# An fp8-rounded cross-attention on one core: two float16 weight parts for three bf16 ones, and the rounding as two bf16 passes on VectorE

## The chip, the cores and the metric

The kernel runs on one core of one Trainium2 chip. The metric is the device time of one execution in microseconds (us), lower is better. A core has five engines that run their own instruction streams and meet only at semaphores: TensorE (PE in the rows; its weight loads are listed as PEld), VectorE (DVE), ScalarE (ACT), GpSimd (POOL) and SyncE (SP), which here only issues transfers.

## The reference

The program is a chain of seven blocks on 2048 tokens of width 256. The change touches one of them, a grouped-query attention whose linear layers see inputs rounded to the float8 e4m3 grid (16 query heads, 8 key groups, head width 128), once over the tokens themselves and once over a conditioning input:

```
def _div_clamp_fp8(x, scale):
    y = jnp.clip(x / scale, -FP8_MAX, FP8_MAX)
    y = y.astype(jnp.bfloat16).astype(jnp.float32)
    return _fp8_roundtrip(y)
def _fp8_linear_pertensor(x, wq, w_scale, in_scale):
    xq = _div_clamp_fp8(x, in_scale)
    return jnp.einsum('bsi,oi->bso', xq * in_scale, wq) * w_scale
...
q  = _ln(_fp8_linear_pertensor(ln_out, wq, wq_scale, q_in_scale) per head, qln_w, qln_b)
k, v, qx likewise (v without _ln);  kx, vx = split(cond @ w_kv_x.T) (kx with _ln)
cat  = concatenate([_gqa(q, k, v), _gqa(qx, kx, vx)])
catq = _div_clamp_fp8(cat, proj_smooth)
return einsum(catq, wproj) * (proj_in_scale * proj_w_scale)
```

The weights `wq`, `wqx`, `wk`, `wv` are float32. Inputs on the fp8 grid are exact in bf16, so a projection keeps float32 accuracy if the weight is split into several 16-bit parts and the products are added.

## The kernel before

The program is a list of stages, each a class with one method for each engine (`sp`, `pe`, `dve`, `act`, `pool`); a barrier of all engines stands between stages. Two stages matter here.

**The mixture-of-experts stage** (`MoeTop6`, about 392 to 582 us for its 32 experts) prepares the attention's weights beside the experts. `Fp8Weights.cuts` are 12 pieces of 128x1024. For each, SP loads the piece into `f_stage`, ScalarE scales it by input scale times weight scale (`scaled`), VectorE takes each head's mean out (`centred`; for `v` only a copy), and the piece is split into three bf16 parts: ScalarE rounds it to part 0 (`first`), VectorE subtracts (`left`), ScalarE rounds to part 1 (`second`), VectorE subtracts to part 2 (`third`). The parts lie in `w3`, which the rows print as `f_w` (numbers in names are left out). `parameters` runs on VectorE ahead of the first expert's product and makes the small vectors (scales, reciprocals).

**The attention stage** (`Fp8Attention`, about 582 to 1432 us) walks through steps `w`. In each step every engine does one unit `u` of four heads (8 units in each of 16 batches of 128 tokens, 128 units in all), each engine a different phase of it: scores of unit u on TensorE, maxima (`f_nmax`) of u-1 on VectorE, exponentials of u-1 on ScalarE, reciprocal of the sums (`sums`) of u-2 on VectorE and the division by them (`divide`, POOL line 3584) of u-2 on GpSimd, transposes of u-3, values and scaling to bf16 (`smooth`, tile `f_cb`) of u-4, rounding to the fp8 grid of u-5. Between these lie the projections of the batches to come, from the table `MADE`: in each step one "early" item (four heads of q or qx), and one "late" item, in even steps of a batch a v or vx with an output product (`o`), in odd ones a k or kx. A projected head item (kind N) goes PE product, ACT squares (`f_sq`), DVE sum of squares (`head_squares`, L3387), POOL power -1/2 (`head_factors`, L3590), DVE scaling out of PSUM (`scale_heads`, L3397), PE transposes. I number the steps of a batch 0 to 7; VectorE handles a late k or kx item of an odd step in the even step behind it. All orders are written out by hand, and each engine follows its own strictly.

The rounding adds and takes away a number 1.5 * 2^20 times the power of two of the value: the sum of a bf16 value and that number is rounded in float32 at the place where e4m3 ends. Before, `round_c` on VectorE clips (`f_cbr`), masks out the exponent (`f_cm`) and multiplies it (`f_cmr`); GpSimd adds in float32 (`round_c_pool`, L3579, tile `f_cf`); VectorE subtracts one step later (`end_c`, L3427). The tiles are laid as three rows of 172 with a gap (516 elements with padding). The same is done for each batch's 128x1024 input in `clip_z`, `round_z` on GpSimd (L3572, 2.1 us) and `end_z` (L3378). A fp8 projection (`project`) is six matmuls of 512 columns: three weight parts by two halves of the 256 inputs.

## Time and profile before

| | us |
|---|---|
| median of 3 runs | 2301.07 (2299.93 to 2303.12) |
| the profiled execution, its own time | 2299.93 |
| its span in the profile | 2298.1 |
| TensorE busy | 1964.0 (85%) |
| VectorE busy | 1788.6 (78%) |
| ScalarE busy | 1382.0 (60%) |
| GpSimd busy | 1170.5 (51%) |
| mean granted TensorE clock | 0.914 of full |

The shares are means over stages of different kinds. To see what bounds the attention stage, read busy times by stretch, then the waits, then the timeline of one batch of it. In the timeline a row is start, duration, engine, line, operation, and in brackets the idle time ahead of it with what ended it. VectorE rows overlap: an instruction that waits for nothing starts some 0.08 us ahead of the recorded end of the one before, so the time that an instruction takes of the engine is the distance of starts.

### The profile page before, as it was taken

How to read it: one execution, taken by the hardware profiler on the slowest of the kernel's cores; microseconds unless marked ns; L12 is line 12 of the kernel's file. 1: busy time of each engine (PE TensorE's matmuls, PEld its weight loads, DVE VectorE, ACT ScalarE, POOL GpSimd, SP SyncE). 2: the span in 40 equal slices, each digit the busy share in tenths (PEclk: the TensorE clock that was granted, in tenths of full speed). 3: DMA queues.
4: the chain of work that ended last, by engine and by line, in shares of the span. 5: the costliest groups of instructions: out<-in, count | busy, mean ns of one | idle time of the engine just before them, and what ended most of it. 6: DMA issues, size and time to landing. Idle time of an engine off the chain costs nothing. (4 is left out here: it accounts for less than half of the span.)

```text
span 2298.1 us, 42233 instructions
## 1 busy us (share of the span) xinstructions
PE 1964.0 (85%) x13247; PEld 1209.8 (53%) x13333; DVE 1788.6 (78%) x4005; ACT 1382.0 (60%) x3523; POOL 1170.5 (51%) x1397
## 2 busy tenths in 40 slices
PE   5999888999589999999999997499478566888878
PEld 3444455666256777676777775366244233333335
DVE  4899767575579999998999886766587698788855
ACT  0777721454278888888888887133166655477753
POOL 3444201442588888888888775132774112333310
PEclk7899979999799999999999999599599876799989
DMA  5576420776220000000000000542698301477610
GB/s 146 146 179 177 124 81 18 245 246 213 63 46 18 21 20 20 19 22 18 20 20 20 11 3 1 198 147 74 192 251 224 107 21 33 113 190 186 169 49 37
DMA packets 258180, 223.18 MB, mean 97 GB/s; under 512 B 36585, under 2 KB 237900, under 8 KB 257708
## 3 DMA queue, kind: packets, MB, share of 16 engines
q1 hardware_dynamic: 234668, 178.72, 28.0%
q0 software_dynamic: 12240, 32.39, 5.5%
q10 hardware_dynamic: 11056, 9.38, 1.3%
q8 instruction: 113, 1.85, 0.3%
q14 instruction: 103, 0.84, 0.1%
HBM read 141.98 MB, written 79.32 MB: 96 GB/s over the span
## 5 line engine op out<-in xcount | busy, mean ns | idle before, releaser
L3270 PE MATMUL bank<-f_w,f_zc 128*128 128x512 bf16 x1074 | 266.8, 383 | 26.3 <-DVE f_zc L3378 18.4
L3590 POOL TENSOR_TENSOR f_hr<-f_hr,half_pow 128x4 f32<-128x4 f32 x192 | 246.1, 1282 | 84.9 <-DVE f_hr L3387 84.8
L965 ACT ACTIVATE a_PT<-bank 128x512 f32<-128x512 f32 x384 | 214.2, 604 | 82.2 <-PE bank L719 77.7
L851 DVE TENSOR_REDUCE a_nm<-bank 128x2 f32<-128x512 f32 x384 | 242.8, 683 | 24.4 <-PE bank L712 18.2
L712 PE MATMUL bank<-a_stack_k,a_stack_q 57*128 57x256 bf16 (+1 forms) x768 | 164.3, 298 | 83.8 <-DVE a_nm L851 46.7
L3482 ACT ACTIVATE f_Pm<-bank,f_nmax 128x128 f32<-128x128 f32 x512 | 182.5, 383 | 73.7 <-DVE f_nmax L3402 73.6
L3270 PEld LDWEIGHTS bank<-f_w,f_zc 128*128 128x128 bf16 x1152 | 112.4, 99 | 121.8 <-issue 25.6
L965 ACT ACTIVATE f_w<-bank 128x512 f32<-128x512 f32 x256 | 141.4, 600 | 46.9 <-PE bank L719 36.3
L851 DVE TENSOR_REDUCE f_w<-bank 128x2 f32<-128x512 f32 x256 | 162.5, 682 | 8.6 <-PE bank L712 7.1
L3397 DVE TENSOR_TENSOR f_raw<-bank,f_hr 128x512 f32<-128x512 f32 x192 | 131.5, 685 | 42.8 <-POOL f_hr L3590 42.8
L3579 POOL TENSOR_TENSOR f_cf<-f_cbr,f_cmr 128x516 f32<-128x516 bf16 x128 | 156.9, 1226 | 12.6 <-DVE f_cb L3427 11.0
L3387 DVE TENSOR_REDUCE f_hr<-f_sq 128x4 f32<-128x516 f32 x192 | 131.3, 684 | 38.7 <-ACT f_sq L3517 36.8
L3494 ACT ACTIVATE f_cb<-bank,f_rsmooth 128x128 bf16<-128x128 f32 x512 | 147.2, 378 | 23.8 <-PE bank L3230 23.8
L719 PE MATMUL bank<-a_stack_q,a_stack_k 60*128 60x256 bf16 (+1 forms) x768 | 154.9, 282 | 6.1 <-ACT a_PT L965 5.6
L1915 POOL DMA_INDIRECT m_xe<-moe_in,m_token x64 | 75.6, 1181 | 164.8 <-DVE m_token L1794 80.9
L3517 ACT ACTIVATE f_sq<-bank 128x512 f32<-128x512 f32 x192 | 116.5, 607 | 62.4 <-PE bank L3270 38.7
L712 PEld LDWEIGHTS bank<-a_stack_k,a_stack_q 57*128 57x128 bf16 (+1 forms) x768 | 59.0, 100 | 178.9 <-DVE a_nm L851 115.0
L3584 POOL TENSOR_TENSOR f_Pm<-f_Pm,f_rs 128x512 f32<-128x512 f32 x128 | 132.6, 1036 | 23.3 <-DVE f_rs L3407 23.3
L3219 PEld LDWEIGHTS bank<-f_KT,f_QT 128*128 128x128 f32 x1024 | 129.3, 192 | 19.9 <-issue 10.5
L3219 PE MATMUL bank<-f_KT,f_QT 128*128 128x128 f32 x1024 | 135.2, 275 | 0.0
L3230 PE MATMUL bank<-f_PT,f_Vv 128*128 128x256 f32 x512 | 132.1, 381 | 2.3 <-ACT f_cb L3494 2.3
L1133 POOL DMA_INDIRECT f_rows<-moe_out,slot x96 | 107.5, 1119 | 45.8 <-ACTq L137 29.8
(410 smaller groups left out, 5108.4 us busy)
## 6 DMA issues: line engine op xcount, KB each, us to landing
o<-a_sums SPq DMA_DIRECT2D x32, 512.0 KB
cut<-a_parts SPq DMA_DIRECT2D x64, 192.0 KB
cut<-a_parts SPq DMA_DIRECT2D x96, 128.0 KB
m_w<-in_w SPq DMA_DIRECT2D x32, 368.0 KB
moe_out<-m_oe ACTq DMA_DIRECT2D x32, 256.0 KB
cut<-f_w SPq DMA_DIRECT2D x32, 192.0 KB, 3.5
cut<-f_w SPq DMA_DIRECT2D x48, 128.0 KB, 2.7
f_w<-cut SPq DMA_DIRECT2D x32, 192.0 KB, 3.6
```

The lines of the kernel that those rows point to most:

```text
L712: x = t.matmul(ps[:, n * D:(n + 1) * D], self.stack_q[rows, i, slot, n * P:(n + 1) * P], self.stack_k[rows, i, slot, :], start=True, stop= ...
L719: x = t.matmul(ps[:, n * D:(n + 1) * D], self.stack_k[rows, i, slot, n * P:(n + 1) * P], self.stack_q[rows, i, slot, :], start=True, stop= ...
L851: v.tensor_reduce(self.nm[:, g % 2, :, at % self.J, at // self.J], self.k.bank[h % 3][:, :].rearrange("p (n m) -> p n m", n=2), AX.X, ALU. ...
L965: a.activation(self.PT[:, h % 8, :, :].rearrange("p m n -> p (m n)"), self.k.bank[3 + h % 3][:, :], ACT.Exp).then_inc(self.a_exp.sem, 1)
L3219: x = t.matmul(ps[:, j * P:(j + 1) * P], self.QT[:, cross, h, :], self.KT[:, cross, h // 2, :], start=True, stop=True)
L3230: x = t.matmul(self.k.bank[7][:, j * 2 * P:(j + 1) * 2 * P], self.Vv[:, cross, n * 2 + j, :], self.PT[:, u % 2, j * 2 * P:(j + 1) * 2 * P] ...
L3270: x = t.matmul(ps[:, :], self.zc[:, b % 2, j, c_, :], self.fp8.w3[:, m, c_, at:at + BANK], start=(m == 0 and c_ == 0), stop=(m == 2 and c_ ...
L3482: x = a.activation(self.Pm[:, i, j * P:(j + 1) * P], ps[:, j * P:(j + 1) * P], ACT.Exp, bias=self.nmax[:, i, j:j + 1], accum_out=self.rs[: ...
L3494: x = a.activation(self.cb[:, u % self.NCB, j * P:(j + 1) * P], ps[:, j * P:(j + 1) * P], ACT.Copy, scale=self.fp8.rsmooth[:, h:h + 1])
L3579: g.tensor_tensor(self.cf[:, :].rearrange("p (r n) -> p r n", r=3), clipped, steps, ALU.add).then_inc(self.g_c.sem, 1)
L3584: g.tensor_tensor(pm, pm, self.rs[:, u % 3, :].unsqueeze(2).to_broadcast([P, self.HPB, P]), ALU.mult).then_inc(self.g_P.sem, 1)
L3590: g.tensor_tensor(f, f, self.k.half_pow[:, 0:self.HPB], ALU.pow).then_inc(self.g_hr.sem, 1)
```

## The change

1. **Weights as two float16 parts.** `w3` (three bf16 parts) becomes `cut_w` (two float16 parts, a third less memory). Each piece loses `left` on VectorE (float32 128x1024) and `second` on ScalarE; `rest` has two buffers for three. A projection is four matmuls for six.
2. **Scaling for float16's range.** `parameters` also loads the input scales as rows (`in_rows`, one more transfer, 512 KB), finds the largest factor of each projection, divides by it and multiplies by 32; the constant under the square root (`least_sq`) is scaled for each kind of head, so `sq` gets a region for each of the four kinds; the scaling of v is taken back in `rsmooth`.
3. **Rounding on VectorE alone, in bf16.** The number added is now 24 times the exponent (in bf16 the sum has 8 bits, which ends where e4m3 does), the addition and the subtraction are bf16 `tensor_tensor` instructions on VectorE, tiles `f_cs`, `f_zs`. GpSimd's additions, their waits, and `end_c` one step later are gone. The tiles are plain 128x512; the five instructions are handed out over the step by a generator (`yield`), between the other work.
4. Memory of the first attention moves (a new tile `spare`), with no instruction added or moved there.

The core of the diff:

```
-            for m in range(3):
+            for m in range(2):
                 for c_ in range(DC):
-                    x = t.matmul(ps[:, :], self.zc[:, b % 2, j, c_, :], self.fp8.w3[:, m, c_, at:at + BANK],
-                                 start=(m == 0 and c_ == 0), stop=(m == 2 and c_ == DC - 1))
+                    x = t.matmul(ps[:, :], self.zc[:, b % 2, j, c_, :], self.fp8.cut_w[:, m, c_, at:at + BANK],
+                                 start=(m == 0 and c_ == 0), stop=(m == 1 and c_ == DC - 1))
...
+    def second(self, v, n):
         v.wait_ge(self.a_w0.sem, self.a_w0.at(n + 1))
-        v.tensor_tensor(x, x, self.part(n, 0), ALU.subtract).then_inc(self.v_rest.sem, 1)
...
+        v.tensor_tensor(self.part(n, 1), self.rest[:, n % 2, :], self.part(n, 0), ALU.subtract).then_inc(self.v_w1.sem, 1)
...
+            c.mark(v.tensor_scalar(self.in_rows[:, j, :], self.in_rows[:, j, :], ws[:, j:j + 1], None, ALU.mult))
...
+        c.mark(v.tensor_reduce(most[:, :], self.in_rows[:, :, :], AX.X, ALU.max, apply_absolute_value=True))
...
+            rounding = self.round_c(v, u - 5) if self.on(u - 5) else iter(())
             if self.on(u - 1):
                 self.maxima(v, u - 1)
+            next(rounding, None)
...
     def round_c(self, v, u):
...
+        at = c.mark(v.tensor_scalar(x, x, FP8_MAX, -FP8_MAX, ALU.min, ALU.max))
+        yield
+        c.after(at)
+        at = c.mark(v.tensor_scalar(m.bitcast(U16), x.bitcast(U16), 0x7F80, None, ALU.bitwise_and))
+        yield
+        c.after(at)
+        at = c.mark(v.tensor_scalar(m, m, 2.0 ** -6, self.GRID, ALU.max, ALU.mult))
+        yield
+        c.after(at)
+        at = c.mark(v.tensor_tensor(sums, x, m, ALU.add))
+        yield
+        c.after(at)
+        v.tensor_tensor(x, sums, m, ALU.subtract).then_inc(self.v_cb.sem, 1)
+        yield
...
+        c.mark(v.tensor_tensor(zs, zb, zm, ALU.add))
+        c.after()
+        v.tensor_tensor(zb, zs, zm, ALU.subtract).then_inc(self.v_z.sem, 1)
...
-    def round_c_pool(self, g, u):
-        g.wait_ge(self.v_cm.sem, self.v_cm.at(u + 1))
-        if u:
-            g.wait_ge(self.v_cb.sem, self.v_cb.at(u))
-        clipped, steps = self.rows_of(u)
-        g.tensor_tensor(self.cf[:, :].rearrange("p (r n) -> p r n", r=3), clipped, steps, ALU.add).then_inc(self.g_c.sem, 1)
```

**VectorE, one even step of a batch in the middle of the attention stage, before.** It has a late k or kx item; `f_nmax` opens the step.

```order
L3402 TENSOR_REDUCE f_nmax<-bank 128x4
L3397 TENSOR_TENSOR f_raw<-bank,f_hr 128x512
L3387 TENSOR_REDUCE f_hr<-f_sq 128x4
L3407 RECIPROCAL f_rs<-f_rs 128x4
L3413 TENSOR_SCALAR f_cbr<-f_cb 128x3x172
L3415 TENSOR_SCALAR f_cm<-f_cbr 128x516
L3417 TENSOR_SCALAR f_cmr<-f_cm 128x3x172
L3397 TENSOR_TENSOR f_raw<-bank,f_hr 128x512
L3387 TENSOR_REDUCE f_hr<-f_sq 128x4
L3427 TENSOR_TENSOR f_cb<-f_cf,f_cmr 128x516
```

The same step after. `f_cs` holds the bf16 sums.

```order
L3414 TENSOR_REDUCE f_nmax<-bank 128x4
L3424 TENSOR_SCALAR f_cb<-f_cb 128x512
L3409 TENSOR_TENSOR f_raw<-bank,f_hr 128x512
L3427 TENSOR_SCALAR f_cm<-f_cb 128x512
L3399 TENSOR_REDUCE f_hr<-f_sq 128x4
L3430 TENSOR_SCALAR f_cm<-f_cm 128x512
L3419 RECIPROCAL f_rs<-f_rs 128x4
L3409 TENSOR_TENSOR f_raw<-bank,f_hr 128x512
L3433 TENSOR_TENSOR f_cs<-f_cb,f_cm 128x512
L3399 TENSOR_REDUCE f_hr<-f_sq 128x4
L3436 TENSOR_TENSOR f_cb<-f_cs,f_cm 128x512
```

Between the late item's `f_hr` and the `f_raw` that needs its power from GpSimd stood four instructions; two are left there (one multiplication and the reciprocal). The two passes for the sum stand around the early item's `f_hr`, behind that `f_raw`.

**GpSimd, an even step (4) and the odd one behind it, before** (`f_Pm` is the division, `f_hr` the power, `f_rows` a gather):

```order
L3579 TENSOR_TENSOR f_cf<-f_cbr,f_cmr 128x516
L3590 TENSOR_TENSOR f_hr<-f_hr,half_pow 128x4
L3584 TENSOR_TENSOR f_Pm<-f_Pm,f_rs 128x512
L3590 TENSOR_TENSOR f_hr<-f_hr,half_pow 128x4
L1133 DMA f_rows<-moe_out,slot 128x256
L3579 TENSOR_TENSOR f_cf<-f_cbr,f_cmr 128x516
L3584 TENSOR_TENSOR f_Pm<-f_Pm,f_rs 128x512
L3590 TENSOR_TENSOR f_hr<-f_hr,half_pow 128x4
```

After:

```order
L3579 TENSOR_TENSOR f_hr<-f_hr,half_pow 128x4
L3573 TENSOR_TENSOR f_Pm<-f_Pm,f_rs 128x512
L3579 TENSOR_TENSOR f_hr<-f_hr,half_pow 128x4
L1134 DMA f_rows<-moe_out,slot 128x256
L3573 TENSOR_TENSOR f_Pm<-f_Pm,f_rs 128x512
L3579 TENSOR_TENSOR f_hr<-f_hr,half_pow 128x4
```

The additions into `f_cf` are gone, and the division follows the late item's power directly.

**TensorE, an even step, before** (`f_w` is the weight tile):

```order
L3219 MATMUL bank<-f_KT,f_QT 128x128 x4
L3270 MATMUL bank<-f_w,f_zc 128x512 x6
L3198 MATMUL bank<-ident,f_Pm 128x128 x4
L3230 MATMUL bank<-f_PT,f_Vv 128x256 x2
L3206 MATMUL bank<-ident,f_raw 128x128 x4
L3263 MATMUL bank<-f_wkv,f_cT 128x512 x2
L3251 MATMUL bank<-f_wproj,f_cb 128x256 x8
```

After:

```order
L3229 MATMUL bank<-f_KT,f_QT 128x128 x4
L3280 MATMUL bank<-f_cut_w,f_zc 128x512 x4
L3208 MATMUL bank<-ident,f_Pm 128x128 x4
L3240 MATMUL bank<-f_PT,f_Vv 128x256 x2
L3216 MATMUL bank<-ident,f_raw 128x128 x4
L3273 MATMUL bank<-f_wkv,f_cT 128x512 x2
L3261 MATMUL bank<-f_wproj,f_cb 128x256 x8
```

The order is the same; the projection has four matmuls for six.

## Rows read from the trace of the kernel before

**Rows 1.** Busy us by stretch; columns: stretch, length, engines, granted clock, DMA share, GB/s
```profile
392.00:582.00 190.00, 181.75 (x792) 126.10 (x792) 111.75 (x162) 79.88 (x132) 75.56 (x64) 1.00 0.70 221
...
689.00:1289.00 600.00, 588.68 (x3512) 421.59 (x3572) 544.89 (x1237) 498.56 (x1596) 519.99 (x445) 1.00 0.08 20
...
1339.00:1387.00 48.00, 47.51 (x284) 34.06 (x288) 38.35 (x78) 40.21 (x131) 32.96 (x29) 1.00 0.00 1
1387.00:1432.00 45.00, 36.47 (x231) 28.22 (x230) 32.21 (x75) 32.98 (x126) 24.70 (x23) 0.94 0.00 1
```

**Rows 2.** Timeline: one batch input's last rounding pass, twelve batches apart
```profile
688.95 1.22 DVE L3378 TENSOR_TENSOR f_zc<-f_rows,f_zm 128x1024 bf16<-128x1024 f32 x1
...
1289.38 1.22 DVE L3378 TENSOR_TENSOR f_zc<-f_rows,f_zm 128x1024 bf16<-128x1024 f32 x1
```

**Rows 3.** Timeline: a whole projection of six matmuls, merged
```profile
940.49 1.46 PE L3270 MATMUL bank<-f_w,f_zc 128*128 128x512 bf16 x6 [0.64 <-DVE f_zc L3378]
```

**Rows 4.** Waits, 689 to 1289 us; columns: us in total, times, longest
```profile
DVE f_raw L3397 <- POOL f_hr L3590: 27.9, 36, 1.2
...
DVE f_hr L3387 <- ACT f_sq L3517: 15.5, 24, 1.0
```

**Rows 5.** Timeline of step 0, an even step, from the late item's squares on
```profile
933.70 0.68 DVE L3387 TENSOR_REDUCE f_hr<-f_sq 128x4 f32<-128x516 f32 x1
...
934.38 0.39 DVE L3413 TENSOR_SCALAR f_cbr<-f_cb 128x516 bf16<-128x516 bf16 x1
934.74 1.17 POOL L3579 TENSOR_TENSOR f_cf<-f_cbr,f_cmr 128x516 f32<-128x516 bf16 x1
...
935.87 1.01 POOL L3590 TENSOR_TENSOR f_hr<-f_hr,half_pow 128x4 f32<-128x4 f32 x1
936.87 1.03 POOL L3584 TENSOR_TENSOR f_Pm<-f_Pm,f_rs 128x512 f32<-128x512 f32 x1
936.92 0.69 DVE L3397 TENSOR_TENSOR f_raw<-bank,f_hr 128x512 f32<-128x512 f32 x1 [1.23 <-POOL f_hr L3590]
937.53 0.68 DVE L3387 TENSOR_REDUCE f_hr<-f_sq 128x4 f32<-128x516 f32 x1
938.12 0.69 DVE L3427 TENSOR_TENSOR f_cb<-f_cf,f_cmr 128x516 bf16<-128x516 f32 x1
938.29 1.39 POOL L3590 TENSOR_TENSOR f_hr<-f_hr,half_pow 128x4 f32<-128x4 f32 x1 [0.39 <-DVE f_hr L3387]
938.73 0.48 DVE L1140 SCALAR_TENSOR_TENSOR X<-f_rows,wts,X 128x256 f32<-128x256 f32 x1
```

**Rows 6.** Timeline of step 1, an odd step: its first instruction, and the one behind L3427
```profile
940.26 0.68 DVE L3402 TENSOR_REDUCE f_nmax<-bank 128x4 f32<-128x512 f32 x1
...
944.35 0.48 DVE L1140 SCALAR_TENSOR_TENSOR X<-f_rows,wts,X 128x256 f32<-128x256 f32 x1
```

**Rows 7.** Timeline of step 3: a subtraction that starts while GpSimd divides
```profile
954.56 1.04 POOL L3584 TENSOR_TENSOR f_Pm<-f_Pm,f_rs 128x512 f32<-128x512 f32 x1
955.07 1.09 DVE L3427 TENSOR_TENSOR f_cb<-f_cf,f_cmr 128x516 bf16<-128x516 f32 x1
```

**Rows 8.** Groups by shape: prices of bf16 passes; columns: busy us, mean ns, idle ahead
```profile
L1773 DVE TENSOR_SCALAR f_w<-f_w 128x384 bf16<-128x384 bf16 x4 | 0.8, 255 | 0.0
...
L3365 DVE TENSOR_SCALAR f_zc<-f_zc 128x1024 bf16<-128x1024 bf16 x1 | 0.4, 421 | 0.0
```

**Rows 9.** One line's instructions, durations ns min/median/max: the last feed-forward's matmuls
```profile
L2874 PE MATMUL bank<-t_xs,w_L_w x192: 379/379/634, 2210.1 to 2284.3; 128*128 128x512 f16 x192
```

**Rows 10.** Timeline of step 1, ScalarE: the late item's squares
```profile
945.63 0.68 ACT L3517 ACTIVATE f_sq<-bank 128x512 f32<-128x512 f32 x1
```

**Rows 11.** Timeline, expert stage: a gather on GpSimd with a copy on VectorE inside it
```profile
528.40 1.55 POOL L1915 DMA_INDIRECT m_xe<-moe_in,m_token  x1 [2.69 <-PE bank L1576]
529.14 0.69 DVE L1239 COPY f_rest<-f_stage 128x1024 f32<-128x1024 f32 x1
```

**Rows 12.** Timeline: VectorE's first product behind the parameters
```profile
405.43 0.88 DVE L1819 TENSOR_TENSOR m_he<-m_sge,bank 128x256 f32<-128x256 f32 x2 [5.70 <-PE bank L1590]
```

More of the change, by code:

```diff
@@ L1168, in allocate_staging @@
         s = lambda name, n: self.k.sb(f"f_{name}", [P, n, self.STG], F32, ctx)
-        self.stage, self.rest = s("stage", 2), s("rest", 3)
+        self.stage, self.rest = s("stage", 2), s("rest", 2)
         self.mean = self.k.sb("f_mean", [P, 2, self.STG // HD1], F32, ctx)
@@ L1211, in parameters @@
         for j in range(4):
-            c.mark(v.tensor_scalar(self.wins[:, j, :], self.ins[:, j, :], ws[:, j:j + 1], None, ALU.mult))
+            c.mark(v.tensor_scalar(self.in_rows[:, j, :], self.in_rows[:, j, :], ws[:, j:j + 1], None, ALU.mult))
+            c.mark(v.tensor_scalar(self.wins[:, j, :], self.ins[:, j, :], ws[:, j:j + 1], W_TOP, ALU.mult, ALU.mult))
+        c.after()
+        c.mark(v.tensor_reduce(most[:, :], self.in_rows[:, :, :], AX.X, ALU.max, apply_absolute_value=True))
+        c.after()
+        c.mark(v.tensor_scalar(most[:, :], most[:, :], FLT_MIN, None, ALU.max))
+        c.after()
+        c.mark(v.tensor_scalar(self.rsmooth[:, 0:HEADS1], self.rsmooth[:, 0:HEADS1], most[:, 3:4], 1.0 / W_TOP, ALU.mult, ALU.mult))
+        c.after()
+        c.mark(v.reciprocal(most[:, :], most[:, :]))
+        c.after()
+        c.mark(v.tensor_tensor(self.least_sq[:, :], most[:, :], most[:, :], ALU.mult))
+        for j in range(4):
+            c.mark(v.tensor_scalar(self.wins[:, j, :], self.wins[:, j, :], most[:, j:j + 1], None, ALU.mult))
+        c.after()
+        c.mark(v.tensor_scalar(self.least_sq[:, 0:3], self.least_sq[:, 0:3], HD1 * EPS * W_TOP * W_TOP, None, ALU.mult))
+        c.mark(v.memset(self.least_sq[:, 3:4], HD1 * EPS))
         for at in (0, 4):
@@ L1658, in dve @@
             if not odd and 0 <= n - 2 < len(self.fp8.cuts):
-                self.fp8.left(v, n - 2)
-            if odd and 0 <= n - 3 < len(self.fp8.cuts):
-                self.fp8.third(v, n - 3)
+                self.fp8.second(v, n - 2)
             if odd and 0 <= n < len(self.fp8.cuts):
@@ L1854, in act @@
             n, odd = divmod(e - 2, 2)
-            if odd and 0 <= n - 2 < len(self.fp8.cuts):
-                self.fp8.second(a, n - 2)
             if not odd and 0 <= n - 1 < len(self.fp8.cuts):
@@ L3282, in dve @@
             u = w - self.PRE
+            rounding = self.round_c(v, u - 5) if self.on(u - 5) else iter(())
             if self.on(u - 1):
                 self.maxima(v, u - 1)
+            next(rounding, None)
             for x in self.early(w - 1):
                 self.scale_heads(v, x)
+            next(rounding, None)
             for x in self.made.get(w - 1, []):
@@ L3336, in prepare @@
         if b is not None:
-            self.clip_z(v, b)
-        b = self.batch(w, self.ROUNDED)
-        if b is not None:
-            self.end_z(v, b)
+            self.round_z(v, b)
     def moments(self, v, b, src):
@@ L3386, in head_squares @@
         v.wait_ge(self.a_sq.sem, self.a_sq.at(n + 1))
-        v.tensor_reduce(self.factors(item), self.sq[:, n % self.NSQ, :, :], AX.X, ALU.add).then_inc(self.v_hv.sem, 1)
+        v.tensor_reduce(self.factors(item), self.squares(item), AX.X, ALU.add).then_inc(self.v_hv.sem, 1)
     def scale_heads(self, v, item):
@@ L3516, in square @@
             a.wait_ge(self.v_hv.sem, self.v_hv.at(n - self.NSQ + 1))
-        a.activation(self.sq[:, n % self.NSQ, :, 0:HD1], self.bank_of[item][:, :].rearrange("p (h d) -> p h d", h=self.HPB),
+        a.activation(self.squares(item)[:, :, 0:HD1], self.bank_of[item][:, :].rearrange("p (h d) -> p h d", h=self.HPB),
                      ACT.Square).then_inc(self.a_sq.sem, 1)
@@ L3557, in pool @@
                 self.power(g, b, 1)
-            b = self.batch(w, self.CLIPPED)
-            if b is not None:
-                self.round_z(g, b)
     def power(self, g, b, n):
@@ L3618, in program @@
                         first.allocate_tail(rest)
+                        spare = k.sb("spare", [P, 5120], F32, rest)
                     experts.allocate()
```

124 lines of the change are left out of this document (50 added, 74 removed).

## The prediction

> **What bounds the kernel now.** I read first the table of stretches, then the waits of the attention stage, then the timeline of one of its batches. The attention stage takes 582 to 1432 us; nearly all that the change does for time lies there. In its regular part, 689 to 1289 us, TensorE is busy 588.7 of 600 us, VectorE 544.9, GpSimd 520.0, ScalarE 498.6, at a granted clock of 1.00 [rows 1]. The same instruction comes at 688.95 and 1289.38 with eleven between: 12 batches, **50.04 us a batch** [rows 2]. TensorE looks like the bound. But VectorE's gaps are few and named: 27.9 us for GpSimd's power of a late item and 15.5 us for ScalarE's squares [rows 4], or 2.3 and 1.3 us a batch. VectorE overlaps neighbours by some 0.08 us, so its busy time (45.4 a batch) and these waits and its short waits for its own results make up the whole 50. Two engines are full, and a change that relieves one has to be counted through the other.
>
> **TensorE.** Six matmuls of 512 columns take 1.46 us of which the last one's own 0.38 is not pitch: (1.46 - 0.38) / 5 = 0.216 us each [rows 3]. The change takes 2 of 6 from 12 projections a batch: 24 x 0.216 = 5.2 us. TensorE alone would then need at most 50.0 - 5.2 = **44.8 us a batch**. float16 moving data costs the same: 379 ns a matmul of the same shape [rows 9].
>
> **VectorE, the prices.** I count from start to start. A 512-element float32 pass takes 0.68 and 0.60 of pitch (937.53 to 938.12) [rows 5]. The three bf16 passes of one input lose the odd layout: 384 elements take 0.255 and 1024 take 0.421 [rows 8], so 512 take 0.29, pitch 0.20, where 516 in three rows take 0.39 [rows 5]. The new two-input bf16 pass has no row. Bounds: 0.29 (the one-input pass) and 0.69 (L3427 in float32) [rows 5, 8]. I take 0.42, pitch 0.34, because L3413, 16 bit in a layout that can't be halved, runs 516 elements in 0.39. For the 1024 form the same way 0.69 (between 0.42 and 1.22 [rows 2, 8]).
>
> The Trainium skill (VectorE: DVE Perf Modes, § The perf-mode tier table) says that a bf16 `tensor_tensor` from SBUF does two elements a cycle; an estimate by it is 0.27 us and the fixed part of some 0.15, 0.42. No run here shows it yet.
>
> **An even step** (step 0). Before, without waits: maxima and early scaling 1.20, then from the late item's sum of squares to the end of the rounding 938.73 - 933.70 = 5.03, less the wait of 1.23, 3.80 [rows 5]; 5.00 a step, 20.0 for four, and 2.3 + 1.3 of waits [rows 4]: 23.6. After: maxima 0.60, clip 0.20, early scaling 0.60, mask 0.20; now the late sum of squares starts, call it 0. The multiplication and the reciprocal end at 0.9. But the late scaling waits for the power on GpSimd, which starts 0.76 after the sum of squares does (937.53 to 938.29) and takes 1.01 (935.87) [rows 5]: it ends at 1.77, the scaling starts at 1.81 and the next could at 2.41. Before, the 1.2 us of rounding covered this latency; **the change takes the cover away**, while it also takes GpSimd's 1.17 us addition out of its way. From 1.77 to 2.80 GpSimd divides (1.03, directly behind the power as at 936.87 [rows 5]). Here the trace has a second cost: a VectorE pass with two SBUF inputs that starts inside the division does not run: 955.07 took 1.09 instead of 0.69, and ended 0.56 after the division's end [rows 7], 0.13 less than its free duration. So the bf16 addition ends at 2.80 + 0.30 = 3.10, the next starts at 3.02; early sum of squares 0.60, bf16 subtraction 0.34: 3.96. Step: 1.60 + 3.96 = 5.56, four 22.2. The wait for ScalarE's squares stays in part: in step 1 they end at 945.63 + 0.68 = 6.05 after that step's maxima [rows 6, 10], with the shorter odd step VectorE asks at 5.9; I keep 0.8 of the 1.3. Together 23.0, a gain of **0.6**.
>
> **An odd step** (step 1). Before: 944.35 - 940.26 = 4.09 [rows 6], four and the stall of 0.4 in step 3 [rows 7]: 16.8. After: 0.60 + 0.20 + 0.60 + 0.20 + 0.40 (output added) + 0.20 = 2.20 up to the reciprocal. From its start: the bf16 addition runs 0.12 to 0.54, ahead of the division, which it holds back: behind a VectorE pass of this kind GpSimd ends 0.87 after the pass does (938.12 + 0.69 = 938.81, 938.29 + 1.39 = 939.68) [rows 5]; so about 1.44. The sum of squares (0.60) runs beside it, then the subtraction is held: it ends 1.74, the next starts 1.66. Step 3.86, four 15.4: a gain of **1.4**.
>
> **The rest of a batch.** The input's rounding: two passes of pitch 0.73 and 0.61 and one more wait for an own result (0.1) against 1.14 of L3378: **-0.3**. The tokens are ready one step earlier and GpSimd's 2.1 us are gone; nobody waits long for either. Sum: 0.6 + 1.4 - 0.3 = 1.7; the other odd and even steps carry some own-result waits that the new order spreads out, which I put at 0.15: **1.85 us a batch, 48.2**. ScalarE (41.5 a batch [rows 1]) and GpSimd (43.3 less 8 x 1.17 and 2.1, 32) stay below. TensorE, with 44.8, waits in gaps under a microsecond; I expect its clock to stay at 1.00.
>
> **Outside the regular part.** The stretch 1339 to 1387 has no input to prepare: VectorE is busy 38.4 of 48, TensorE 47.5 [rows 1], and it has the full 72 projection matmuls, so it follows TensorE's 5.2 down until ScalarE (40.2) binds: 4. The last unit run, 1387 to 1432, is a chain of rounding (1.3 us of bf16 passes, 1.17, 0.69, two waits in place of which come 1.8): 2. The fill, 582 to 643, is latency: three passes, GpSimd's 2.1 and L3378's 1.2 give way to 1.4, and the first projections have four matmuls: 3. The stretch 643 to 689: 2. In the expert stage VectorE loses 12 passes of 1.2 us and ScalarE 12 of 1.0, but TensorE is busy 181.8 of 190 us there [rows 1]: 0. `parameters` grows by four 256-element passes (0.3 each), a reduction of 1024 (1.2) and some ten small ones with waits, 4.9 us; VectorE idles 5.70 us ahead of its first product [rows 12]: covered, by less than 1 us. The row load of 512 KB is issued while no transfer is urgent: 0.
>
> **Sum** against the profiled execution: 2299.93 - 13 x 1.85 - 4 - 2 - 3 - 2 = 2299.93 - 35 = 2265. That execution stands 1.1 us under the median of 2301.07: 2266; I say **2265**.
>
> **Rivals.**
> *TensorE binds (20%).* If the new passes are not held by the division, and the power comes sooner, the VectorE batch is 48.2 less the holds, (0.27 + 0.29) x 4 = 2.3, and less the squares' wait, 45.1: TensorE's 44.8 decides. 13 x 5.2 + 5 + 5 + 2 + 6 = 86 at most: 2215. For it: TensorE's share; against: the 1.09 us row [rows 7].
> *The two-input pass runs at float32's rate (7%), slower.* At 0.69 in place of 0.42 each of 16 passes adds 0.26 to its step, and the holds don't absorb it, since they end with the division: 4.2, and the two input passes 1.1: 53.5 a batch, 13 x 3.4 = 45 longer, less 7 outside: 2338. It decides from about 0.52 us a pass (18 x 0.1 eats the 1.85).
> *Gathers hold the clip and the mask (5%), slower.* Six gathers of 1.1 us a batch lie where these two now run. If a gather held VectorE's one-input passes of the halved kind as the division holds L3427, the mask would wait some 0.5 us six times: 51.2 a batch, 2300 + 15 - 9 = 2306. Against it: the copy at 529.14, 1024 float32 elements in 0.69 where a full-rate pass needs 1.22, ran inside a gather at its usual time [rows 11].
> The Trainium skill (SBUF — State Buffer, § Who interferes with whom) states the general rule, a two-port VectorE mode and GpSimd exclude each other for the whole instruction; a page's rule that would give this rival's time. The copy's row does not show it for a gather.
> *Gain and new waits cancel (10%)*: ScalarE's squares and the power come later than I laid them by 0.25 a step: 2296 to 2304.
> Forecast case: 58%, 2245 to 2290.
>
> **How the numbers follow.** Range 2215 to 2302: it leaves out the slower cases and the edge of the TensorE one, some 20%. A difference under 0.2% is about what a measurement of this kernel can't tell from none. Faster by more: 58 + 20 = 78%; within: 10%; slower: 12%.
>
> **What would show it.** Right: 48 us between two input roundings; TensorE busy about 93% of them at clock 1.00; the bf16 addition near 0.42 free and up to 0.8 where it starts inside a division; a wait of `f_raw` for `f_hr` of some 0.8 us four times a batch; no GpSimd addition. Wrong: TensorE still 98% busy (then the division doesn't hold), two-input passes at 0.68, clips above 0.3 us beside gathers, or VectorE's first product later than 405.4 us.

## The result, and the profile after

| | before | after |
|---|---|---|
| median, us | 2302.1 (4 runs, 2299.93 to 2306.65) | **2270.83** (4 runs, 2259.74 to 2274.26) |
| ratio | | **0.984**, 95% interval 0.981 to 0.988 |
| the profiled execution, its span | 2299.93, 2298.1 | 2274.26, 2272.5 |
| mean granted clock of it | 0.914 | 0.902 |
| attention stage, from the start of its first `memset` to the start of the last addition into X | 848.3 | **816.7** |
| one regular batch | 50.04 | **48.46** |

2265 was predicted, 2215 to 2302 as the range. Busy time by stretch, columns as in [rows 1]: the regular part, and the two stretches at the stage's end.

```profile
690.00:1272.00 582.00, 536.81 (x3296) 393.26 (x3295) 531.95 (x1345) 485.01 (x1597) 360.51 (x336) 1.00 0.08 20
...
1319.00:1367.00 48.00, 47.19 (x296) 35.23 (x295) 39.05 (x95) 43.64 (x145) 23.84 (x22) 1.00 0.00 1
1367.00:1409.00 42.00, 35.93 (x232) 27.76 (x230) 36.08 (x89) 34.00 (x129) 11.85 (x10) 1.00 0.00 1
```

TensorE is busy 92% of the regular part, where it was 98% [rows 1], VectorE 91%. The end of a batch input's rounding, timeline of VectorE, eleven batches apart:

```profile
739.04 0.69 DVE L3388 TENSOR_TENSOR f_zc<-f_zs,f_zm 128x1024 bf16<-128x1024 bf16 x1
...
1272.13 0.69 DVE L3388 TENSOR_TENSOR f_zc<-f_zs,f_zm 128x1024 bf16<-128x1024 bf16 x1
```

(1272.13 - 739.04) / 11 = 48.46 us a batch, against 50.04 [rows 2]. VectorE's waits between 690 and 1272 us (us in total, times, longest), which answer to [rows 4]:

```profile
DVE f_raw L3409 <- POOL f_hr L3579: 41.3, 48, 0.9
DVE f_hr L3399 <- ACT f_sq L3527: 4.4, 12, 0.4
```

Four times in each of 12 batches VectorE waits 0.83 to 0.88 us for GpSimd's power: 3.4 us a batch, where it was 2.3. The waits for the squares fell from 1.3 to 0.4. An even step from the late item's power on, timeline of GpSimd and VectorE, as [rows 5]:

```profile
984.33 1.01 POOL L3579 TENSOR_TENSOR f_hr<-f_hr,half_pow 128x4 f32<-128x4 f32 x1 [4.48 <-DVE f_hr L3399]
...
985.31 1.03 POOL L3573 TENSOR_TENSOR f_Pm<-f_Pm,f_rs 128x512 f32<-128x512 f32 x1
985.37 0.69 DVE L3409 TENSOR_TENSOR f_raw<-bank,f_hr 128x512 f32<-128x512 f32 x1 [0.83 <-POOL f_hr L3579]
985.97 0.65 DVE L3433 TENSOR_TENSOR f_cs<-f_cb,f_cm 128x512 bf16<-128x512 bf16 x1
...
987.15 0.41 DVE L3436 TENSOR_TENSOR f_cb<-f_cs,f_cm 128x512 bf16<-128x512 bf16 x1
```

The bf16 addition starts inside the division (985.31 to 986.34) and ends 0.28 behind it, at 986.62; the subtraction, free, takes 0.41. The odd step and the start of the even one behind it:

```profile
990.18 0.43 DVE L3433 TENSOR_TENSOR f_cs<-f_cb,f_cm 128x512 bf16<-128x512 bf16 x1
990.31 1.19 POOL L3573 TENSOR_TENSOR f_Pm<-f_Pm,f_rs 128x512 f32<-128x512 f32 x1 [1.89 <-DVE f_rs L3419]
...
991.22 0.57 DVE L3436 TENSOR_TENSOR f_cb<-f_cs,f_cm 128x512 bf16<-128x512 bf16 x1
...
992.83 1.12 POOL L1134 DMA_INDIRECT f_rows<-moe_out,slot  x1 [0.18 <-issue]
...
993.50 0.54 DVE L3427 TENSOR_SCALAR f_cm<-f_cb 128x512 uint16<-128x512 uint16 x1
```

Here the addition comes first and lengthens the division (1.19 for 1.03), and the subtraction meets it. The last row was not in my main sum: a mask takes 0.54 instead of 0.28 and ends 0.09 behind a gather's end (993.95). In twelve batches 24 of 96 masks and 24 of 96 clips do so, four passes a batch. All of them start 0.43 to 0.46 us ahead of a gather's end. A clip that starts earlier in a gather, and a mask that starts still later, run free:

```profile
999.07 1.09 POOL L1134 DMA_INDIRECT f_rows<-moe_out,slot  x1 [0.18 <-issue]
999.27 0.28 DVE L3424 TENSOR_SCALAR f_cb<-f_cb 128x512 bf16<-128x512 bf16 x1
...
1000.08 0.28 DVE L3427 TENSOR_SCALAR f_cm<-f_cb 128x512 uint16<-128x512 uint16 x1
```

**Ahead of the attention stage the profiled execution of the changed kernel lost 10 us** (the stage starts at 592.2, before at 582.3). The stretch is one that the diff doesn't touch. The same kernel was profiled again (e10 below). One stretch of both profiles, first that of the table above, then e10's:

```profile
270.00:335.00 65.00, 56.18 (x290) 35.33 (x282) 30.94 (x95) 21.53 (x37) 2.80 (x3) 0.53 0.34 110
```

```profile
270.00:335.00 65.00, 55.63 (x337) 37.41 (x336) 40.92 (x124) 22.31 (x39) 2.59 (x3) 0.74 0.34 109
```

At a granted clock of 0.53 (nearly all of it at 1.2 GHz) against 0.74 the second had done more of its work by 335 us, and its attention stage started at 579.4. Over the 14 profiled executions of this case the stage started nine times at 579 to 582 us, with a granted clock of 0.71 to 0.76 between 270 and 335 us, and five times at 589 to 592, with 0.53 to 0.56; the changed kernel is in both groups. So medians of few runs carry some 10 us that no kernel made, and below I read the attention stage and the batch first: they repeat (48.46 and 48.49 us, 816.7 and 815.9).

### The profile page after: what moved, and what is told of

It is laid out like the page before. It is cut to its first block and busy times, and to the rows that moved or that the text cites. A ratio compares the mean times of both kernels' runs of the same rounds, so it can differ in the third digit from the quotient of the medians.

```text
span 2272.5 us, 41321 instructions
## 1 busy us (share of the span) xinstructions
PE 1915.8 (84%) x12949; PEld 1178.3 (52%) x12949; DVE 1763.4 (78%) x4155; ACT 1355.3 (60%) x3511; POOL 959.4 (42%) x1253
## 5 line engine op out<-in xcount | busy, mean ns | idle before, releaser
L3579 POOL TENSOR_TENSOR f_hr<-f_hr,half_pow 128x4 f32<-128x4 f32 x192 | 215.4, 1122 | 192.1 <-DVE f_hr L3399 191.6
L3280 PE MATMUL bank<-f_cut_w,f_zc 128*128 128x512 f16 x768 | 202.5, 388 | 14.0 <-DVE f_raw L3409 7.8
L3573 POOL TENSOR_TENSOR f_Pm<-f_Pm,f_rs 128x512 f32<-128x512 f32 x128 | 142.6, 1114 | 111.9 <-DVE f_rs L3419 111.9
L966 ACT ACTIVATE f_cut_w<-bank 128x512 f32<-128x512 f32 x256 | 141.7, 600 | 51.6 <-PE bank L720 41.0
L852 DVE TENSOR_REDUCE spare<-bank 128x2 f32<-128x512 f32 x256 | 162.4, 681 | 8.8 <-PE bank L713 7.4
L3504 ACT ACTIVATE f_cb<-bank,f_rsmooth 128x128 bf16<-128x128 f32 x512 | 153.7, 431 | 5.2 <-PE bank L3240 3.5
L3216 PE MATMUL bank<-ident,f_raw 128*128 128x128 f32 x768 | 114.8, 277 | 42.4 <-ACT f_PT L3484 41.3
L3527 ACT ACTIVATE f_sq<-bank 128x512 f32<-128x512 f32 x192 | 121.1, 631 | 43.8 <-PE bank L3273 22.1
L3273 PE MATMUL bank<-f_wkv,f_cT 128*128 128x512 f32 x256 | 123.2, 606 | 6.2 <-DMA f_cT<-in_ctx_T 5.9
L3216 PEld LDWEIGHTS bank<-ident,f_raw 128*128 128x128 f32 x768 | 91.3, 142 | 69.3 <-issue 55.9
```

The source lines that it names most:

```text
L852: v.tensor_reduce(self.nm[:, g % 2, :, at % self.J, at // self.J], self.k.bank[h % 3][:, :].rearrange("p (n m) -> p n m", n=2), AX.X, ALU. ...
L966: a.activation(self.PT[:, h % 8, :, :].rearrange("p m n -> p (m n)"), self.k.bank[3 + h % 3][:, :], ACT.Exp).then_inc(self.a_exp.sem, 1)
L3216: x = t.transpose(ps[:, h * P:(h + 1) * P], self.raw[:, n % self.NRAW, h * HD1:(h + 1) * HD1], self.k.ident[:, :])
L3280: x = t.matmul(ps[:, :], self.zc[:, b % 2, j, c_, :], self.fp8.cut_w[:, m, c_, at:at + BANK], start=(m == 0 and c_ == 0), stop=(m == 1 and ...
L3504: x = a.activation(self.cb[:, u % self.NCB, j * P:(j + 1) * P], ps[:, j * P:(j + 1) * P], ACT.Copy, scale=self.fp8.rsmooth[:, h:h + 1])
L3573: g.tensor_tensor(pm, pm, self.rs[:, u % 3, :].unsqueeze(2).to_broadcast([P, self.HPB, P]), ALU.mult).then_inc(self.g_P.sem, 1)
```

## Experiments

Batch, stage and median of all (batch: between two input roundings in the regular part; ratio to the kernel before on the same chip):

| kernel | batch | stage | median | ratio, 95% |
|---|---|---|---|---|
| before | 50.04 | 848.3 | 2302.1 | |
| changed | 48.46 | 816.7 | 2270.8 | 0.984 (0.981 to 0.988) |
| e1 weight parts, GpSimd rounds the output | 49.73 | 832.7 | 2287.1 | 0.995 (0.992 to 0.998) |
| e2 six matmuls | 49.29 | 836.5 | 2291.0 | 0.994 (0.990 to 0.997) |
| e3 two matmuls | 48.5 / 50.1 | 819.2 | 2270.7 | 0.989 (0.982 to 0.995) |
| e4 short division (part of the work left out) | 47.20 | 799.4 | 2246.3 | 0.977 (0.971 to 0.982) |
| e5 passes in the power's shadow | 46.68 | 792.7 | 2242.7 | 0.974 (0.970 to 0.977) |
| **e6 passes ahead of the reciprocal** | **45.97** | **783.1** | **2232.7** | **0.969** (0.965 to 0.972) |
| e7 = e6, six matmuls | 48.92 | 831.7 | 2279.5 | 0.991 (0.986 to 0.996) |
| e8 = e6, two matmuls | 45.9 / 46.9 | 785.4 | 2234.5 | 0.973 (0.967 to 0.980) |
| e9 early reciprocal | 47.00 | 795.5 | 2239.3 | 0.972 (0.969 to 0.975) |
| e10 changed, again | 48.49 | 815.9 | 2269.6 | 0.987 (0.983 to 0.990) |
| e11 plain rows for gathers (other rows) | 48.23 | 809.9 | 2252.4 | 0.978 (0.975 to 0.982) |
| e12 = e6, plain rows (other rows) | 45.74 | 776.9 | 2222.4 | 0.966 (0.961 to 0.970) |

My theory, theory A in the expectations: VectorE's chain, with its waits for GpSimd, sets the batch on both sides of the change. The first rival, theory B: TensorE set it, and the weight parts carry the gain.

### e1, e2, e3: each part alone, and TensorE's load

e1 is the changed kernel with `round_c`, `end_c` and `round_c_pool` of before:

```diff
-            rounding = self.round_c(v, u - 5) if self.on(u - 5) else iter(())
+            if self.on(u - 5):
+                self.round_c(v, u - 5)
...
+            if self.on(u - 6):
+                self.end_c(v, u - 6)
```

> The change with the rounding of the attention's output as before the change (three one-input passes in three rows, addition on GpSimd, L3427-type subtraction in float32); the two float16 weight parts and the rounding of the inputs on VectorE stay. Theory A (VectorE's chain sets the batch, TensorE only waits for it): a batch of 49.3 to 49.8 us, since VectorE gets back its passes and keeps only the 0.3 us of the inputs' rounding and a part of the 1.3 us of waiting for ScalarE's squares; 2283 us (2278 to 2292). Theory B (the weight parts carry the gain, TensorE was the bound): 44.8 to 46.5 us a batch, 2225 to 2247 us.

49.73 us a batch: theory A. With 24 matmuls fewer in each batch TensorE was busy 91% and the batch hardly moved.

e2 and e3 change only the parts' loop in `project`, and the `stop` flag of its last matmul with it (the comments are mine):

```diff
-            for m in range(2):
+            for m, last in ((0, False), (1, False), (1, True)):   # e2
+            for m in range(1):                                    # e3
```

> The changed kernel with six matmuls a projection instead of four: the second weight part is multiplied twice, so TensorE has its load of before the change and VectorE the new rounding (the projections come out a rounding error of the weights off). TensorE is now busy 461.2 of 500 us, 44.7 us a batch of 48.46; 24 more matmuls of 0.216 us are 5.2: 49.9. If both engines stand at the edge as I hold, the batch becomes 50 us and the kernel about 2297 us (2292 to 2303): the new rounding alone would be worth nearly nothing. If TensorE were far from binding even then: 48.5 us and 2271 us.

49.29, 0.6 to 0.7 less than expected, with TensorE full; the median of 2291 stands just under the expected range. The regular part (700 to 1200 us) of e2, and of e7, which has the same matmuls in the better order:

```profile
700.00:1200.00 500.00, 498.86 (x3026) 356.76 (x3024) 447.20 (x1134) 422.59 (x1352) 305.26 (x285) 1.00 0.07 20
```

```profile
700.00:1200.00 500.00, 500.00 (x3047) 360.27 (x3046) 450.12 (x1148) 425.49 (x1362) 302.39 (x287) 1.00 0.08 20
```

TensorE is shown busy all the time in both, at 49.29 and at 48.92 us a batch, so busy time alone doesn't give its need. With six matmuls that need is at most e7's **48.92 us**, 1.1 under the 50.04 of before: VectorE's chain was the longer of two nearly equal ones. The rounding alone can give no more than the distance between them (e2: 0.75), the weight parts alone only what VectorE lets through (e1: 0.31, and that came with the inputs' rounding on VectorE), together 1.58. That is 0.5 more than the two gains added. Some 0.3 of it is the longer rounding of the inputs, which e1 and e2 both carry and the whole carries once; only about 0.2 is left for each part uncovering the other engine. e6 and e7 below show that effect at its full size.

> The changed kernel with two matmuls a projection: the second weight part is left out of the product. TensorE would need 39.5 us a batch. Theory A (VectorE's chain with its waits for GpSimd sets 48.46): 48.2 to 48.5 us a batch, and only the stretch without inputs to prepare and the fill get shorter, 2260 to 2271 us. Theory B (TensorE still sets the pace by when it delivers): 43 to 46 us a batch, 2200 to 2240 us.

Seven of the twelve batches took 48.47, five 50.1. VectorE's chain stands, theory A; but the emptier TensorE cost time. Stretches of one of the long batches, and VectorE's wait behind them:

```profile
902.00:904.50 2.50, 0.39 (x5) 0.40 (x5) 2.50 (x8) 2.50 (x11) 1.00 (x1) 1.00 0.19 56
904.50:907.00 2.50, 2.50 (x10) 1.41 (x9) 2.50 (x6) 2.14 (x6) 2.31 (x3) 0.63 0.00 0
907.00:909.50 2.50, 2.50 (x11) 1.45 (x10) 0.53 (x2) 0.94 (x4) 0.13 (x1) 0.68 0.18 52
```

```profile
909.19 0.69 DVE L3399 TENSOR_REDUCE f_hr<-f_sq 128x4 f32<-128x516 f32 x1 [1.97 <-ACT f_sq L3527]
```

TensorE was busy 0.39 of 2.5 us, its granted clock then averaged 0.63 and 0.68 (in part at 1.2 GHz, in part at 2.4), the projection came late, and VectorE waited 1.97 us for its squares. Each of the five long batches has one such drop, 3.4 us at 1.2 GHz, and none of the seven short ones has. The stage took 819.2 us, longer than with twice the matmuls, and the median is the changed kernel's.

### e4: what the division holds

```diff
-        g.tensor_tensor(pm, pm, self.rs[:, u % 3, :].unsqueeze(2).to_broadcast([P, self.HPB, P]), ALU.mult).then_inc(self.g_P.sem, 1)
+        g.tensor_tensor(pm[:, :, 0:1], pm[:, :, 0:1], self.rs[:, u % 3, :].unsqueeze(2), ALU.mult).then_inc(self.g_P.sem, 1)
```

> The changed kernel with GpSimd's division of the probabilities cut to one element of 128 in each head (the other probabilities stay undivided; that part of the computation is left out), all waits kept. Theory A (a two-input bf16 pass that meets the division waits for its end, and GpSimd's power of an early item queues behind it): the additions of the even steps and the subtractions of the odd steps fall from about 0.65 to 0.42, and their queues with them, 8 times 0.24 to 0.29, or 1.9 to 2.3 us a batch: 46.2 to 46.6 us a batch, 2240 to 2248 us. Rival (these passes are long for another reason, such as ScalarE's traffic): their durations stay at 0.65 and the batch at 48.0 to 48.5, 2265 to 2271 us.

Durations (ns, min/median/max) of the bf16 addition and subtraction, one line's view each, were 424/537/665 and 407/562/664; now:

```profile
L3433 DVE TENSOR_TENSOR f_cs<-f_cb,f_cm x84: 412/421/427, 704.4 to 1193.8; 128x512 bf16<-128x512 bf16 x84
```

```profile
L3436 DVE TENSOR_TENSOR f_cb<-f_cs,f_cm x84: 411/416/419, 705.3 to 1194.8; 128x512 bf16<-128x512 bf16 x84
```

The division took 0.19 to 0.36 us instead of 1.03 to 1.19, and the passes are free: the hold is the division's. The batch fell by 1.26, not 1.9 to 2.3: the surplus durations were 4 x 0.23 and 4 x 0.15 to 0.25, 1.6 in all, and waiting for the squares grew from 3.6 to 8.0 us in 500, 0.4 a batch.

### e5, e6: the cover given back

In e6 the addition and the subtraction stand behind the multiplication and ahead of the reciprocal. e5 has them behind the reciprocal.

```diff
             for x in late:
                 self.head_squares(v, x)
             next(rounding, None)
+            next(rounding, None)
+            next(rounding, None)
             if self.on(u - 2):
                 self.sums(v, u - 2)
             for x in late:
                 self.scale_heads(v, x)
-            next(rounding, None)
             for x in self.early(w):
                 self.head_squares(v, x)
-            next(rounding, None)
```

> The changed kernel with both two-input bf16 passes moved between the reciprocal and the scaling of the late item, same work. In the changed kernel's batch VectorE waits 0.83 to 0.88 us four times for the power of the late item, and runs the addition and the subtraction (0.34 each) behind that wait. Theory A (the wait is what the lost cover costs): the two passes fill it, and the held additions (0.22 us more each, even steps) go too, since they now start ahead of the division: 4 x (0.8 + 0.2), 4 us less a batch, but not under TensorE's 44.7: 44.7 to 46 us a batch instead of 48.46, 2220 to 2237 us on this chip. Rival (GpSimd's power is itself held by the VectorE passes beside it and comes later by what they take): the wait comes back, 47.5 to 48.5 us a batch, 2258 to 2271 us. Second rival: the subtractions of the odd steps, now directly behind the additions, meet the division and hold everything behind them: 46.5 to 47.5.

> As the run with both two-input bf16 passes moved ahead of the late scaling, but they stand ahead of the reciprocal too, so that in no step a division can run beside them. Theory A: no pass is held (all at 0.42), the wait of 0.83 us for the power is covered; against it the division starts 0.7 us later in each step, and who waits for the divided probabilities gets them later. 44.7 to 46 us a batch if that has slack (GpSimd is busy 63%), 2218 to 2237 us; 47 to 48.5 us and 2250 to 2271 us if the late division moves the power of the early item, which queues behind it, onto VectorE's path.

An even step of e6, from the power on:

```profile
966.86 1.01 POOL L3579 TENSOR_TENSOR f_hr<-f_hr,half_pow 128x4 f32<-128x4 f32 x1 [4.09 <-DVE f_hr L3399]
967.01 0.43 DVE L3433 TENSOR_TENSOR f_cs<-f_cb,f_cm 128x512 bf16<-128x512 bf16 x1
967.48 0.43 DVE L3436 TENSOR_TENSOR f_cb<-f_cs,f_cm 128x512 bf16<-128x512 bf16 x1
...
967.91 0.69 DVE L3409 TENSOR_TENSOR f_raw<-bank,f_hr 128x512 f32<-128x512 f32 x1
968.07 1.04 POOL L3573 TENSOR_TENSOR f_Pm<-f_Pm,f_rs 128x512 f32<-128x512 f32 x1 [0.20 <-DVE f_rs L3419]
```

Both passes run while GpSimd computes the power, and the late scaling follows without a wait. The work of this even step took 4.61 us, in the changed kernel 5.52. e5 gains the same there, but its 46.68 missed the 44.7 to 46 of its theory and fell in the range of its second rival. It loses in the odd steps, where the subtraction meets the division (1.15 us for 0.43):

```profile
977.62 1.19 POOL L3573 TENSOR_TENSOR f_Pm<-f_Pm,f_rs 128x512 f32<-128x512 f32 x1 [1.69 <-DVE f_rs L3419]
977.94 1.15 DVE L3436 TENSOR_TENSOR f_cb<-f_cs,f_cm 128x512 bf16<-128x512 bf16 x1
```

In e6 the division of an odd step meets the addition of a gathered row instead (0.91 for 0.47 us, three times a batch), the smaller loss: 45.97, at the upper end of the 44.7 to 46 expected. It is the fastest kernel here that computes all of the reference: 1.6% under the changed kernel by the two ratios (1.8% by e10's), 3.2% under the kernel before.

### e7, e8: what binds e6

> The order with both two-input bf16 passes ahead of the reciprocal (45.97 us a batch), with six matmuls a projection: the second weight part is multiplied twice, so TensorE has its load of before the change. With this load the changed kernel took 49.29 us a batch with TensorE busy 498.9 of 500 us. Theory (that was TensorE's own need): again 49.2 to 49.4 us a batch, 12 x 3.3 us and some 10 us outside longer than the 2233 us of this order, 2278 to 2290 us; the weight parts are then worth 3.3 us a batch here and 0.8 in the change's order. Rival (49.29 was made of both engines' waits for each other): the better order shows here too, 47.5 to 48.7 us a batch, 2255 to 2270 us.

> The order with both two-input bf16 passes ahead of the reciprocal, with two matmuls a projection: the second weight part is left out. Theory (VectorE's own work, busy 483.8 of 500 us, now sets 45.97 us a batch, and TensorE's 96% busy is waiting with it): 45.8 to 46.0 us a batch where the granted clock stays at 1.00, up to 1.6 more in batches where it falls, as in the run with one product in the change's order; 2222 to 2240 us. Rival (TensorE has become the bound): 42 to 44.5 us a batch, under 2215 us.

e7 gave 48.92, between the theory (49.2 to 49.4) and the rival (47.5 to 48.7): most of e2's 49.29 was TensorE's need, and 0.37 of it came from the order. With the better order the weight parts are worth 2.95 us a batch, in the change's own order 0.83 (49.29 - 48.46). e8 gave 45.95 in four batches and 46.9 in eight, each with 3.4 us at 1.2 GHz. With two matmuls fewer a projection the short batches are no shorter than e6's: VectorE's own work binds e6.

### e9: an attempt that lost

In odd steps the reciprocal moves up behind the clip, and the subtraction stays behind the early sum of squares; even steps have e5's order. The cut shows the reciprocal's move.

```diff
+            if not late and self.on(u - 2):
+                self.sums(v, u - 2)
             for x in self.early(w - 1):
                 self.scale_heads(v, x)
```

> The changed kernel in the order of the first better one in the even steps (both two-input bf16 passes between the reciprocal and the late scaling), and in the odd steps the reciprocal moved up behind the clip, so that the division starts some 2 us earlier and runs beside passes that read PSUM, the subtraction behind the early sum of squares. Theory (in the order with the passes ahead of the reciprocal the division of an odd step holds the addition of a gathered row behind it, 0.91 instead of 0.47 us three times a batch, and once the 0.40 us pass of L3336, 0.77): 45.97 - 3 x 0.44 - 0.37 = 44.3 us a batch, but TensorE's own need is 44.3 to 44.7 too, so 44.5 to 45.1; 13 times 1.2 less than 2232.7, 2213 to 2222 us. Rival (ScalarE's exponentials of the row come too late for an early reciprocal, and VectorE waits there): 46 us a batch or more, 2232 us.

47.00 us a batch and 2239 us, a miss for the theory, and the rival's cause isn't it either. ScalarE wasn't waited for; the mask, a pass of one input, met GpSimd:

```profile
987.55 1.09 POOL L1134 DMA_INDIRECT f_rows<-moe_out,slot  x1 [0.18 <-issue]
...
988.46 1.96 DVE L3431 TENSOR_SCALAR f_cm<-f_cb 128x512 uint16<-128x512 uint16 x1
988.68 0.58 POOL L3572 TENSOR_TENSOR f_mv<-f_mv,half_pow 128x1 f32<-128x1 f32 x1
989.23 1.04 POOL L3577 TENSOR_TENSOR f_Pm<-f_Pm,f_rs 128x512 f32<-128x512 f32 x1
```

It waited through the gather's end, a small power and the whole division: 1.96 us instead of 0.28. With only the division beside it the mask took 0.65 to 1.09, the more the earlier in the division it started. I had counted only passes of two inputs as held.

### e10, e11, e12: the loss ahead of the stage, and the gathers

> The changed kernel once more, beside the kernel before on another chip. Its attention stage should again take 817 us (48.46 us a batch); if the 10 us that the profiled run of it lost ahead of that stage belong to the run and not to the kernel, its attention stage may start at 580 us here as well as at 592, and the median should stand some 30 us under that of before (2265 to 2275); if they belong to the kernel, it starts at 592 again.

The stage started at 579.4: the 10 us belong to the run.

In e11 and e12 plain transfers of fixed rows take the place of the gathers, so these two compute with other rows than the reference does:

```diff
-        at = bass.IndirectOffsetOnAxis(ap=self.slot[:, b, j:j + 1], axis=0)
-        g.indirect_dma_start(rows[:, j, :], None, self.k.obuf, at, bounds_check=SLOTS, oob_is_err=False).then_inc(self.d_row[j].sem, 16)
+        g.dma_start(rows[:, j, :], self.k.obuf[(j + 1) * P:(j + 2) * P, :]).then_inc(self.d_row[j].sem, 16)
```

> The changed kernel with GpSimd's indirect gathers of expert rows (1.07 to 1.12 us each, six a batch) replaced by plain transfers of 128 rows from the same queue; the rows are others, so the input of the attention is, too. Theory (of the 192 clips and masks in 12 batches 48 take 0.53 instead of 0.28, each of them started in the last 0.5 us of a gather: the gather holds them): all clips and masks take 0.28, and a batch gets up to 4 x 0.25 = 1.0 us shorter, less what comes back as waiting for ScalarE's squares (up to 0.4): 47.4 to 47.9 us a batch, 2256 to 2263 us. Rival (they are long for another reason, or lie under the waits for GpSimd's power): 48.3 to 48.5 us a batch, 2268 to 2271 us.

> The order with both two-input bf16 passes ahead of the reciprocal (45.97 us a batch), with plain transfers in place of the gathers (other rows). There the clips and masks that meet a gather lose only 0.05 to 0.08 us, some three times a batch each: 45.6 to 45.9 us a batch by the durations. If GpSimd, 6.6 us a batch emptier, also lets the division of the odd steps end earlier, the held additions of rows (0.91 instead of 0.47) may shorten: down to 45.0. Slower than 46 if the emptier GpSimd only moves its divisions under other VectorE passes.

The mask in the changed kernel, and in e11:

```profile
L3427 DVE TENSOR_SCALAR f_cm<-f_cb x83: 275/281/540, 702.7 to 1199.2; 128x512 uint16<-128x512 uint16 x83
```

```profile
L3426 DVE TENSOR_SCALAR f_cm<-f_cb x83: 274/280/288, 704.6 to 1199.5; 128x512 uint16<-128x512 uint16 x83
```

So the long masks and clips were the gathers' doing. But the batch gained only 0.23, since in the even steps, where three of the four stood, the waits for ScalarE's squares came back: 3.6 us in 500 before, 11.4 now. 48.23 lies just under the rival's 48.3 and above the theory's 47.4 to 47.9: the durations were as the theory had them, the price was not. e12 gave 45.74, the middle of what the durations said. The stages of e11 and e12 are 6.8 and 6.2 us shorter, of which 13 x 0.23 explains 3; another 1.7 and 2.3 lie between the first two input roundings, and why is open.

## Why the prediction was right, point by point

**The sum.** 35 us were predicted as 24 in the regular part and 11 outside; the stage gave 31.6, of which 13 x 1.58 = 20.5 in the regular part and 11.1 outside. That the outside comes out is in part luck, since its terms don't. Measured between the maxima that open the batches (`f_nmax`), the fill up to the first of them was 5.3 us shorter (3 predicted), the next stretch 2.4 us longer (2 shorter predicted), the last stretch with an input 2.9 shorter (1.85), the one without an input 3.7 shorter (4), and the rest of the stage 3.2 shorter (2).

**The batch** gained 1.58 us for 1.85. One batch of each kernel, divided at the end of each step's own work (what follows is preparation of inputs and the gathered rows):

| | before | after | gain | predicted |
|---|---|---|---|---|
| four even steps | 23.7 | 23.4 | 0.3 | 0.6 |
| four odd steps | 17.1 | 15.6 | 1.5 | 1.4 |
| the rest | 9.2 | 9.5 | -0.25 | -0.3 |
| own-result waits | | | in the rows above | 0.15 |

**The prices held.** The two-input bf16 pass takes 0.41 to 0.43 free (0.42 taken between bounds of 0.29 and 0.69), the one of 1024 elements 0.69, the one-input pass 0.28 (0.29). The rival at float32's rate is dead. The estimate by the Trainium skill (VectorE: DVE Perf Modes, § The perf-mode tier table) was 0.42 too; the trace agrees.

**TensorE.** 24 matmuls were priced at 5.2 us; by busy time it was 49.1 - 44.7 = 4.4 a batch. "At most 50.0" for TensorE alone is now at most 48.92 (e7). Its clock stayed at 1.00 in the regular part, as said. That it doesn't bind the changed kernel is shown by e3: half its projection matmuls gone, and the batches without a drop of the clock still take 48.47. That six matmuls would have bound a quicker VectorE is shown by e7.

**Even steps.** Predicted 22.2 and 0.8 of waiting for squares, 23.0; the four took 5.52, 5.84, 5.76 and 6.27 up to the next work of `prepare`, 23.4. The power's wait (0.83 to 0.88), the hold by the division (end 0.28 behind it, 0.30 taken) and the clean step of 5.52 (5.56) are as worked out. Three of the four passes held by gathers lie in these steps, 0.26 us each, and the waiting for squares fell to 0.4 us a batch, not 0.8.

**Odd steps.** Predicted 15.4, measured 3.84, 3.84, 4.09 and 3.83: 15.6. The 4.09 is one clip held by a gather. The four of before took 17.1, not the 16.8 of the sum, which took step 1 four times and 0.4 for the stall in step 3: that step took 4.71, 0.6 more than step 1, and step 7 took 4.22.

**The inputs' rounding** cost 0.3 more, as said. "Nobody waits long" for GpSimd's 2.1 us addition of the inputs was wrong for one place: with it gone, step 0 of e1 no longer waits 1.23 us [rows 5] for the power. In the changed kernel the lost cover hides that.

**The step that failed** is the rival on the gathers, and with it the reading of [rows 11]. I took the copy at 529.14, unharmed inside a gather, as evidence that gathers don't hold VectorE. "Clips above 0.3 us beside gathers" was named as a sign of being wrong, and 24 of 96 clips showed it. In the changed kernel the clips that start 0.2 us into a gather run free, the clips and masks that start 0.63 to 0.79 us into it (0.43 to 0.46 ahead of its end) end 0.09 behind its end, and the masks that start 1.0 us into it run free again: the hold lies in a gather's last part, short of its very end. The copy started 0.81 us ahead of its gather's end and was done 0.12 ahead of it. In e9 eight masks that started 0.62 to 0.63 us into a gather of 1.07 were done 0.16 ahead of its end, free, while four that started at the same place took 0.54. That the copy slipped through because it was done in time fits this; it is not shown. The rival's price (six times 0.5) was too high: four times 0.25, and only 0.23 of it reached the batch. In the kernel before, no VectorE pass that started inside a gather was lengthened. Without gathers the batch gains 50.04 - 48.23 = 1.81 of the 1.85 predicted. So most of the miss in the regular term (1.58 for 1.85) is the gathers; the kernel before was not run with plain rows.

The Trainium skill (SBUF — State Buffer, § Who interferes with whom) says that the one of VectorE (in a two-port mode) and GpSimd which comes first keeps the ports for the whole instruction, and that a VectorE instruction with two inputs in SBUF contends with a GpSimd instruction that reads SBUF. For the division the trace agrees (a mask of 0.28 took 0.65 to 1.96 in e9, a bf16 addition of 0.42 took 0.65). Inside a gather a VectorE pass is held only in the last part, and beside the power of 1.01 us the bf16 additions of e6, two inputs in SBUF, took 0.43, as free: there the measurement decides.

**Parameters** stayed covered but for a little. VectorE ahead of the experts in e10, whose clock is nearer to that of before:

```profile
395.43 0.19 DVE L1214 RECIPROCAL f_rins<-f_ins 128x8 f32<-128x8 f32 x1
...
402.85 0.88 DVE L1829 TENSOR_TENSOR m_he<-m_sge,bank 128x256 f32<-128x256 f32 x2 [2.33 <-PE bank L1602]
```

It still waits 2.33 us for TensorE (5.70 before [rows 12]), and the product starts 7.42 us behind the reciprocal, before 6.86. In the profile of the table above it starts at 416.40, later than the 405.4 that the prediction named as a sign of being wrong; but the reciprocal starts 8.9 us late there too, the loss told above, and VectorE still waits 3.81 us. From the first reciprocal to the attention stage it took 184.0 us in e10 and 184.8 there, before 183.7: the experts' stage gained nothing by the passes taken from it, as predicted.

**The median.** 2265 was worked out from an execution at clock 0.914. The two of the changed kernel at 0.914 and 0.915 took 2260.2 and 2259.7, the six at 0.902 to 0.911 took 2267.6 to 2274.3: the 5.8 us between 2265 and the median are less than this spread. At the clock of before, then, the kernel is 40 us shorter and not 35. In e10 the stage gives 32.4 of them, its earlier start 2.9, and the work behind the stage 4.5, which no edit touches and which takes 855 to 869 us in the 14 profiles. So the stage fell short of the forecast, and time that the change doesn't touch made up for it: luck.
